# Second edge stage of a graph transformer: rows multiplied by the weights before the gather, sums kept by node

## What is computed

```python
xn = _layernorm(x)
# graph part
summed = segment_sum(xn[src], dst, n)
deg = segment_sum(ones_like(src), dst, n)
agg = summed / maximum(deg, 1.0)[:, None]
out = concatenate([xn, agg], -1) @ weight      # weight is 512 x 256
out = out / norm(out, axis=-1) + bias
# attention part: q, k, v of xn; kv = sum over nodes of k^T v; ret = q kv + xn; gelu(ret w1) w2 + xn
x = x + graph + attention
# experts: three products with norms and relu, 8 experts, softmax weights of the mean
x = x + experts(layernorm(x))
```

## Time and profile before

| | |
|---|---|
| Median of 3 runs | 2891.04 us (2889.53 to 2899.61) |
| Span of the profiled execution | 2911.8 us |
| TensorE busy | 2563.1 us, 88% |
| VectorE busy | 1693.7 us, 58% |
| ScalarE busy | 1330.1 us, 46% |
| POOL busy | 1185.6 us, 41% |
| Gathers of the second edge stage | 392, 381.6 us of POOL |

### The profile page before, as it was taken

One profiled execution on the slowest core, in us unless ns is written; L12 is line 12 of the kernel. 1 busy time (PEld: TensorE's weight loads), 2 busy tenths in 40 slices (PEclk: granted clock), 3 DMA queues, 4 the chain that ended last, 5 costly groups with the idle time before them and its releaser, 6 DMA issues. The chain is left out here.

```text
span 2911.8 us, 47805 instructions
## 1 busy us (share of the span) xinstructions
PE 2563.1 (88%) x16831; PEld 2377.1 (82%) x16831; DVE 1693.7 (58%) x4350; ACT 1330.1 (46%) x2855; POOL 1185.6 (41%) x1326
## 2 busy tenths in 40 slices
PE   6788899899989998998995999549899999998998
PEld 6778898889888988885675888439898888898898
DVE  4566777677766776555666232355556444444665
ACT  3234565455545554445532122212245454444687
POOL 1223453345434543456840222366654455554100
PEclk9889999999999999998985899856889899999899
DMA  4211112111211120124214444332221232233011
GB/s 106 66 37 37 37 44 66 37 37 43 68 37 37 42 68 23 47 55 107 83 54 118 151 143 139 117 108 84 86 87 38 71 97 84 86 95 92 21 45 29
DMA packets 137166, 205.25 MB, mean 70 GB/s; under 512 B 35134, under 2 KB 98430, under 8 KB 136803
## 3 DMA queue, kind: packets, MB, share of 16 engines
q1 hardware_dynamic: 99842, 107.97, 12.4%
q0 software_dynamic: 37088, 94.23, 11.8%
HBM read 168.50 MB, written 33.62 MB: 69 GB/s over the span
## 5 line engine op out<-in xcount | busy, mean ns | idle before, releaser
L922 POOL DMA_INDIRECT gat<-table,srcT x400 | 412.8, 1032 | 359.0 <-DVE m L2640 259.4
L1066 POOL DMA_INDIRECT x_rows<-table,srcT x392 | 381.6, 974 | 306.4 <-PE pg L1834 146.7
L588 PE MATMUL pa<-w,act 128*125 128x256 f32 x2400 | 362.3, 289 | 12.4 <-DVE act L2399 11.9
L588 PE MATMUL pb<-hT,w 128*128 128x378 f32 (+1 forms) x1920 | 342.3, 315 | 10.9 <-ACT gf L1905 8.5
L588 PEld LDWEIGHTS pa<-w,act 128*125 128x125 f32 x2400 | 317.5, 189 | 17.3 <-DVE act L2399 16.5
L2154 ACT ACTIVATE gf<-pb,bne 128x378 f32<-128x378 f32 (+1 forms) x320 | 194.2, 607 | 252.7 <-PE pb L588 137.5
L588 PEld LDWEIGHTS pb<-hT,w 128*128 128x128 f32 x1920 | 291.7, 192 | 14.9 <-ACT gf L1905 6.4
L1905 ACT ACTIVATE gf<-pb,b1s 128x378 f32<-128x378 f32 (+1 forms) x320 | 165.9, 519 | 139.7 <-PE pb L588 93.8
L2399 DVE TENSOR_TENSOR act<-gf,act 128x378 fp32r<-128x378 f32 (+1 forms) x320 | 153.7, 483 | 102.6 <-ACT act L1908 66.1
L588 PE MATMUL pb<-act,fw 128*128 128x378 f32 (+1 forms) x960 | 169.7, 329 | 29.2 <-ACT gf L2154 28.7
L588 PEld LDWEIGHTS pb<-act,fw 128*128 128x128 f32 x960 | 152.6, 202 | 31.9 <-issue 31.9
(11 more groups left out here) (492 smaller groups left out, 5694.9 us busy)
## 6 DMA issues: line engine op xcount, KB each, us to landing
e<-in_L_ffn_W_dram SPq DMA_DIRECT2D x40, 512.0 KB, 4.6
spill<-m SPq DMA_DIRECT2D x80, 170.0 KB
msg<-spill SPq DMA_DIRECT2D x40, 340.0 KB, 2.9
yslots<-yo SPq DMA_DIRECT2D x64, 128.0 KB, 2.0
fraw<-in_L_ffn_W_dram SPq DMA_DIRECT2D x32, 256.0 KB
w1r<-in_L_mix_W_dram SPq DMA_DIRECT2D x7, 1024.0 KB, 4.9
gat<-table,srcT POOLq DMA_INDIRECT x400
x_rows<-table,srcT POOLq DMA_INDIRECT x392
```

Of the source, the lines that this page charges most:

```text
L588: mm = nc.tensor.matmul(ps, lhs(l), rhs(r), start=first and n == 0, stop=last and n == 2)
L922: pool.indirect_dma_start(out=gat[:, i % 2, c, :], out_offset=None, in_=table0, in_offset=bass.IndirectOffsetOnAxis(ap=srcT[:, i * GC + c: ...
L1066: pool.indirect_dma_start(out=x_rows[:, n % UB, c, :], out_offset=None, in_=table1, in_offset=bass.IndirectOffsetOnAxis(ap=srcT[:, at:at + ...
```

## The change

The rows are multiplied by `aw` before they are stored: each tile gets a `table_product` of six matmuls in the table stage, ScalarE copies the result as upper part and VectorE subtracts it for the lower part. `table1` has rows of 2 KB, with both parts. The gathers are as many as before, of twice the bytes. The work is cut into 98 groups of UG = 4 blocks in a ring of UB = 2, 60 of them for the lower ten tiles and 38 before. TensorE takes the one-hot (128 edges x 125 nodes) as stationary operand and the parts of the rows (256 columns) as the moving one, both fp32r, 8 matmuls a group, each one record. A group can touch two neighbouring slots of 125 nodes; VectorE adds its sum twice into `acc1`, now nodes by features, each time scaled by a mask of the nodes that belong to that slot (`side`). The products with `aw` and the ScalarE copy leave the heads. The key/value stage has one group per tile, the ret stage one per unit, the bursts one, one, one and two groups in each four m. The split of `awx` (the parts of `aw`) stands in the expert stage of the first layer, that of `awo` in the key/value stage; all norms of the table stage are applied on ScalarE; 14 warm-up matmuls (L1609) go; stage 1 makes the slot, the position and the masks of each group. The scratch for POOL's transfers is set to 4096.

The core of the diff:

```diff
-UB = 5
+UG = RR
+UB = 2
...
-    table1 = dram("table1", (N, D))
+    table1 = dram("table1", (N, 2 * D))
...
-    acc1 = sb("acc1", [P, H, NP], F32, s78)
+    acc1 = sb("acc1", [TP, NT + 1, D], F32, s78)
...
-    x_rows = sb("x_rows", [P, UB, UC, D], F32, s78)
+    x_rows = sb("x_rows", [P, UB, UG, 2 * D], R32, s78)
+    oh1 = sb("oh1", [P, UB, UG, TP], R32, s78)
...
     def burst(m):
-        k = NUA + m // 2 * UBP + m % 2 * (UBP - UBU)
-        return range(k, k + (UBU if m % 2 else UBP - UBU)) if m < NMA else range(0)
+        k = NGA + m // 4 * 5 + m % 4
+        return range(k, k + (2 if m % 4 == 3 else 1)) if m < NMA else range(0)
...
+        def fetch_groups(groups):
+            for n in groups:
+                if n >= UB:
+                    pool.wait_ge(s["win_ps"], NPR + n - UB + 1)
+                for c in range(UG):
+                    at = edge_group(n) * UG + c
+                    pool.indirect_dma_start(out=x_rows[:, n % UB, c, :].bitcast(F32), out_offset=None, in_=table1,
...
+        def table_product(t):
+            pe.wait_ge(s["t_lo"], T_L1 + t + 3)
+            pe.wait_ge(s["y_used"], Y_TAB + t + 1)
+            for h in range(H):
+                last = hi_lo_products(pa[0:TP, t % 3, 0:D], lambda l: xT[l][:, t // GT, h, t % GT * TS:t % GT * TS + TP],
+                                      lambda r: awx[r][:, h, :], h == 0, h == H - 1)
+            last.then_inc(s["y_ps"], 1)
...
+        def group_sums(n, to):
+            pe.wait_ge(*rows_landed(n))
+            pe.wait_ge(s["o1_ready"], n + 1)
+            for c in range(UG):
+                for k in range(2):
+                    last = nc.tensor.matmul(to, oh1[:, n % UB, c, :], x_rows[:, n % UB, c, k * D:(k + 1) * D],
+                                            start=c == 0 and k == 0, stop=c == UG - 1 and k == 1)
+            last.then_inc(s["win_ps"], 1)
...
-            for k in range(H):
-                last = nc.tensor.matmul(pa[0:TP, h % 3, 0:D], acc1[:, k, t * TP:(t + 1) * TP], aw[:, k, :],
-                                        start=k == 0, stop=k == H - 1)
...
+            nc.scalar.activation(trow1[:, t % GT, 0, :], pa[0:TP, t % 3, 0:D], ACT.Copy).then_inc(s["tr_hi"], 1)
...
+            nc.vector.tensor_tensor(trow1[:, t % GT, 1, :], pa[0:TP, t % 3, 0:D], trow1[:, t % GT, 0, :], ALU.subtract).then_inc(s["y_used"], 1)
...
+            for k in range(2):
+                to = acc1[:, k:k + NT, :][:, bass.ds(at, 1), :].rearrange("p o d -> p (o d)")
+                nc.vector.scalar_tensor_tensor(to, sums, side[:, 1 - k, g:g + 1], to, ALU.mult, ALU.add).then_inc(s["win_used"], 1)
...
-                nc.scalar.activation(g1[:, n % G_RING, :], pb[0:TP, n % 2, 0:D], ACT.Copy).then_inc(s["act9"], 1)
...
-    nc = _bacc.Bacc("TRN2", target_bir_lowering=False, num_devices=1)
+    nc = _bacc.Bacc("TRN2", target_bir_lowering=False, num_devices=1, dynamic_dma_scratch_size=4096)
```

More of the change, by code:

```diff
@@ L1619, in _ @@
         with pe.If(rest_flag(pe) == 1):
[L1620 removed]
+            with pe.Fori(0, NU * NT) as w:
                 for c in range(UC):
                     pe.wait_ge(s["rb_oh"], w * UC + (c + 1))
[L1623 to L1625 removed]
+                    for k in range(2):
+                        last = nc.tensor.matmul(pb[0:TP, 0, 0:D], ohs1[:, 0:TP], x_rows[:, 0, c, k * D:(k + 1) * D],
+                                                start=c == 0 and k == 0, stop=c == UC - 1 and k == 1)
@@ L3215, in window_start @@
                 regs = nc.values_load_multi_w_load_instructions(
-                    base_i[0:1, pair(n):pair(n) + k], engines=[mybir.EngineType.DVE], min_val=0, max_val=N - 1,
-                    skip_runtime_bounds_check_because="stage 1 clamps every window's start to 0..N - 1")[1]
+                    slot_i[0:1, edge_group(n):edge_group(n) + k], engines=[mybir.EngineType.DVE], min_val=0, max_val=NT - 1,
+                    skip_runtime_bounds_check_because="stage 1 makes it from a count of NT - 1 comparisons")[1]
                 for i in range(k):
```

377 lines of the change are left out of this document (211 added, 166 removed).

## The result

Measured side by side on one chip in 17 runs each, the changed kernel takes 2882.85 us (2872.70 to 2891.54) and the kernel before 2892.36 us; the ratio is 0.9965 (95% interval 0.9954 to 0.9977). That is 9.5 us or 0.35% less. The direction was right, the size is less than half of the 20.5 us that was forecast, and it lies within the 0.5% that the prediction called "the same", though the interval leaves out 1. The profiled execution has a span of 2870.9 us (its own time is 2872.7).

A forecast was written before the change was run, and what follows sets the result against it. Gathers and a chain through engines bound the table stage, TensorE the ret stage; ring and TensorE pace key/value, TensorE and late signals the bursts. 8 + 17 - 7 - 5.5 - 5 - 28 = -20.5, so 2870.5 us, range 2836 to 2914.

The forecast's parts named there:

- Stage 1, +8: Start of the program: longer VectorE chain turning edge indices into positions costs 8 us; ends +4 and +10.
- Table stage, +17: Table stage to first sums: products, splitting and bigger store before the first gather cost 17 us; ends +10 and +28.
- Key/value stage, -7: Key/value stage: 6.4 us a tile against 6.7, limited by the ring, saves 7 us; ends -20 and +34.
- Ret stage, -5.5: Ret stage, bound by TensorE: ten times two units become one group, saving 5.5 us.
- Heads, -5: Heads before each expert half: four matmul records and a copy go, VectorE limits the gain to 5 us; ends 0, -21.
- Bursts, -28: Expert stage with bursts: TensorE's lighter sums save 35 us, 7 taken back for gathers and ring; ends 0 and -79.
- Rival (a): Bursts: small ring becomes the bound, 2886.5 us, chance 0.22; sign: TensorE waits over 2 us in each fourth m.
- Rival (b): Edge gathers: doubled rows slow fetches, key/value stage +30 us, bursts gain nothing; 2935.5 us, chance 0.16.
- (c): Bursts: signals come sooner with gathers in fours, half of the 79 us goes too; 2831 us, chance 0.12.
- (d): Key/value stage: relieved TensorE runs at 1.2 GHz throughout, +10 us in place of -7; 2887.5 us, chance 0.10.

The follow-up runs named there:

- e5: The changed kernel without edit, run again on a chip with late signals: 2904.18 against 2923.54 us for the kernel before, ratio 0.9924.
- halved ring: Changed kernel with tile-by-tile table store, ring freed and awaited by halves: 2734.56 against 2748.78 us for the kernel before, without late signals.
- half rows: Changed kernel with gathers bringing only the rows' upper part, used twice: 2756.08 us, ratio 1.0035 to the kernel before, without late signals.

## Why the prediction was right and wrong

*Stage 1, +8.* Measured +8.2 on every chip.

*Table stage, +17: wrong, and this is the step that failed.* Measured +28.6 in the first pair (90.0 to 118.6 us from the first expert-row gather to the first sums) and +25.8 on the prompt chip. The chain after the last row scales is 22.0 us to the first gather where I had 18 or 19; without the 3.61 us that ScalarE waits for a store in it, 18.4. The price of the last store, +2 for twice the bytes, was right too: 6.0 us where it took 4.0. What I had not priced is that the first four groups of tiles, put down at nothing because gathers stood beside them, share one buffer with their store: "a wait of ScalarE for the store" was a part of 1.5 us. Each group's first copy waits for the store of the group before (5.32 and 3.61 us for the last two), and the first of these waits went up the queue of ScalarE into VectorE (4.96 us), which came to the row scales 14.3 us after the last gather and not 6.9; the rest of the 7.4 us goes with VectorE's own new subtractions between. Storing tile by tile takes 12.9 us back on the prompt chip, where the stage had lost 25.8.

*Key/value stage, -7.* Measured -15.7 on the first chip, and two parts of the term were off. The 167.8 us that I divided by 25 hold 26 pairs of units, 6.45 us each and not 6.7; so my 6.4 left no gain, where I took 7. The stage has 28 such pairs, now 28 groups. And the ring's period, which I put at 6.1 to 6.6 us, is 5.8 (163.2 us for 28 groups; before 6.4), since from the end of a group's sums to POOL's next gather there are 2.3 us on average (0.3 to 3.9) and not 3 or 4; a group's matmuls cost 0.95 at the full clock. On the prompt chip the stage is 4.4 us longer: there a pair took 5.2 us, and a group needs 5.4, of which four gathers are 5.0. My ends of -20 and +34 held both.

*Ret stage, -5.5.* Measured -6.0, and -4.2 on the prompt chip.

*Heads, -5.* Measured -2.5 together (+1.2 and -3.7), and not for the reason I gave. VectorE was to be the bound; in the first head TensorE works without a gap at 2.95 us a tile, at a clock of 0.60 where it had 0.91 (0.67 and 0.90 in the second). In the first head what the missing matmuls save was paid back by the clock. It is so on the prompt chip as well: 0.62 where it was 0.93, and 45.1 us both times.

*Bursts, -28.* The two profiles give -46.8, but their spans overstate the difference of the medians by 31 us (7 of them in the first layer, which is the same program). The other terms make +12.6; so by the medians the bursts gave about -22 on the first chip, and, with the same +12.6 and a difference of 19, -32 on the late chip of e5. That split is worked out, not shown; it takes the other stages to be the same in every execution. On the prompt chip they gave -12.2, with no late signals at all. Rival (a) named the cause: the ring. In the fourth m a fetch is 9.2 us in the rows above, between the 7.7 that I had without a late signal and the 10.7 with one, and 8.5 on the prompt chip (to 2302.37). TensorE waits for rows there, 2.0 us on average in the first profile, just at the sign of "over 2" that I had set for (a); on the prompt chip it waits 1.27 us there and 0.67 in the next m. The halved ring earned 17 us there. The ring took back more of TensorE's 35 us than the 7 I had put down: 13 on the first chip by the split above, 23 on the prompt one.

*Rival (b)*, doubled bytes, has its place in the bursts but not its size: 9 us in the bursts, none in the key/value stage. The estimate by the Trainium skill ("DMA: Bandwidth & Descriptors", "Anatomy of one DMA — SWDGE (gpsimd) path") of 0.3 us more for a fetch isn't contradicted: half rows shortened each four m by 0.7 us, with five fetches in it. *(c)*, signals sooner, happened in part: remote waits from 88.4 to 19.8 us. *(d)*, the clock, did not happen where I had it: 0.78 in the key/value stage where it was 0.70, though TensorE is busy for less of it. It happened in the heads. As I applied the rule of the Trainium skill ("TensorE: Matmul & The Clock Gate", "What's actually happening"), less work should have meant less clock; the measurement decides: it did in the heads and did not in the key/value stage.

In sum, on the first chip: table +11.6, key/value -8.7, heads +2.5, bursts +6, ret -0.5 against the forecast, 11 us in all, which is the error. The table stage alone is as large as the error; that the misses of the other terms nearly cancel is luck.

## What to carry to other kernels

A new step that is hidden beside other work has to be followed to its buffer as well: ask what must land before the buffer is written again, on which queue that wait stands, and what is behind it. A buffer written and stored as a whole delayed twice here, at its first writer and at its last reader; stored piece by piece it did not. And when a saving on one engine is paid for with a shallower ring, price the fetch (issue, landing, signal) against the time between two uses before counting the saving. Read the granted clock of a stage that is relieved of matmuls, too: in the heads it took the saving back.

## What the runs showed that was not expected

The same program runs 6% apart on different chips (2746.66 and 2923.54 us), and a change can win on one kind and lose on the other: 0.9924 and 1.0073. The late signals come where POOL issues gathers in a row; how much of the 6% they make isn't shown. From the kernel before on the first chip, the product of TensorE that ScalarE needs, the last gather of a row of six, and ScalarE:

```profile
2300.85 1.57 PE L588 MATMUL pb<-xT,fw 128*128 128x252 f32 x12
...
2303.57 0.94 POOL L1066 DMA_INDIRECT x_rows<-table,srcT  x1 [0.30 <-issue]
...
2305.87 0.56 ACT L2154 ACTIVATE gf<-pb,bne 128x252 f32<-128x252 f32 x1 [4.32 <-remote]
```

TensorE is done at 2302.42 and ScalarE is released 3.4 us later, when the row has ended. ScalarE's waits of this kind last up to 4.4 us in the bursts, and VectorE's in the first layer, beside longer rows of that layer's gathers, up to 8.4. Breaking the rows of the kernel before by 1.5 us gave 0.9953 on a late chip and 1.0213 on a prompt one. Why chips differ stays open; no run here tells.
